# Two experts per token found with VectorE's eight-largest and position-search instructions, on one Trainium2 core

## The reference, cut to what matters

```python
x = x + 0.5 * _L0_ffn_ref(_layernorm(x), ...)    # f0: 8 experts, hidden 176, 2 per token
x = x + _L0_attn_ref(_layernorm(x), ...)         # h: gated linear recurrence
x = x + 0.5 * _L0_ffn_ref(_layernorm(x), ...)    # f0 again
x = x + 0.5 * _L1_ffn_ref(_layernorm(x), ...)    # f1: 16 experts, hidden 128, 2 per token
x = x + _L1_attn_ref(_layernorm(x), ...)         # a: attention
x = x + 0.5 * _L1_ffn_ref(_layernorm(x), ...)    # f1 again
```

```python
scores = sigmoid(x @ gate_w)                # (T, E)
_, idx = top_k(scores + bias, 2)
w = take_along_axis(scores, idx)            # without the bias
w = w / sum(w)                              # f0: clipped at 1e-12; f1: 1e-20 added
```

## Time and profile before

| | |
|---|---|
| median of 3 runs | 845.12 us (844.83 to 847.11) |
| profiled execution, its own time | 842.05 us |
| its span | 840.1 us |
| TensorE busy | 738.6 us (88%) |
| VectorE busy | 481.7 us (57%), 1816 instructions |
| ScalarE busy | 403.6 us (48%) |
| GpSimd busy | 281.0 us (33%) |

### The profile page before, as it was taken

How to read it: one execution, slowest core, us unless ns; L and a number is a source line. 1 busy time by engine, 2 the same in 40 slices (tenths; PEclk the granted TensorE clock), 3 DMA queues, 4 the chain that set the end, 5 groups by cost and what they waited for, 6 DMA issues and landing times.

```text
span 840.1 us, 13928 instructions
## 1 busy us (share of the span) xinstructions
PE 738.6 (88%) x3946; PEld 497.3 (59%) x3946; DVE 481.7 (57%) x1816; ACT 403.6 (48%) x963; POOL 281.0 (33%) x296
## 2 busy tenths in 40 slices
PE   5999999989898999999966899997899888799970
PEld 3446777554465456777543378666667665378640
DVE  5663333478866663333379653335997866753336
ACT  3822433317643722333246436543788777436530
POOL 0572333400000572433306725550011133635550
PEclk9999999999999999999985999999999999899995
DMA  8843333199999943333195245526000011245528
GB/s 301 270 169 119 106 108 104 58 300 351 351 350 350 352 145 119 105 110 105 58 368 219 107 124 166 156 94 200 1 1 1 2 54 41 94 126 171 155 95 300
DMA packets 99295, 134.62 MB, mean 160 GB/s; under 512 B 11494, under 2 KB 88294, under 8 KB 98662
## 3 DMA queue, kind: packets, MB, share of 16 engines
q1 hardware_dynamic: 85782, 95.97, 36.5%
q0 software_dynamic: 13440, 37.77, 12.2%
HBM read 54.85 MB, written 78.84 MB: 159 GB/s over the span
## 4 chain that ended last, share of the span: by engine, by line
PE 66%; DVE 16%; ACT 7%; DMA 4%; issue 4%; POOL 1%; SPq 0%; POOLq 0%; DVEq 0%; ACTq 0%
PE bank L1030 19%; PE bank L1051 11%; PE bank L926 11%; PE bank L1003 4%; PE bank L939 3%; PE bank L1040 3%; PE bank L1113 3%; DVE X L1348 2%; DVE st L1366 2%; DVE X L1352 2%; PE bank L1164 2%; PE bank L866 2%; DMA Y<-f_result_rows 2%; PE bank L1232 1%; PE bank L1140 1%
## 5 line engine op out<-in xcount | busy, mean ns | idle before, releaser
L517 POOL DMA_INDIRECT f_result_rows<-arena x152 | 146.2, 962 | 209.2 <-ACT arena L676 195.5
L517 POOL DMA_INDIRECT slot_rows<-XN,slots x128 | 123.9, 968 | 239.2 <-DVE slots L1480 177.8
L1030 PE MATMUL bank<-w,arena 128*128 (+3 forms) x800 | 176.9, 417 | 2.2 <-ACT arena L661 0.7
L1668 DVE COPY arena<-bank 88x128 f32<-88x128 f32 (+1 forms) x224 | 56.1, 284 | 155.8 <-PE bank L1040 148.7
L1030 PEld LDWEIGHTS bank<-w,arena 128*128 128x128 f32 (+1 forms) x800 | 103.9, 164 | 41.5 <-issue 15.7
L926 PE MATMUL bank<-XT,f_s 128*128 128x512 f32 (+1 forms) x256 | 122.9, 628 | 1.6 <-ACT arena L676 1.0
L1051 PE MATMUL bank<-w,arena 88*128 (+3 forms) x576 | 118.3, 380 | 1.6 <-DVE arena L1668 1.6
L669 ACT ACTIVATE arena<-bank 128x128 f32<-128x128 f32 (+1 forms) x152 | 45.1, 296 | 106.7 <-PE bank L1030 105.7
L676 ACT ACTIVATE arena<-bank 128x256 f32<-128x256 f32 x152 | 58.5, 385 | 59.6 <-PE bank L1051 59.3
L926 PEld LDWEIGHTS bank<-XT,f_s 128*128 128x128 f32 (+1 forms) x256 | 48.3, 197 | 58.5 <-issue 55.7
L1051 PEld LDWEIGHTS bank<-w,arena 88*128 88x128 f32 (+3 forms) x576 | 71.1, 167 | 14.8 <-issue 4.3
(11 more groups left out here) (178 smaller groups left out, 1078.5 us busy)
## 6 DMA issues: line engine op xcount, KB each, us to landing
slot_rows<-zeros SPq DMA_DIRECT2D x16, 2312.0 KB, 20.1
arena<-slot_rows SPq DMA_DIRECT2D x104, 136.0 KB
XN<-f_result_rows SPq DMA_DIRECT2D x32, 256.0 KB, 5.5
Y<-f_result_rows SPq DMA_DIRECT2D x32, 256.0 KB, 6.0
arena<-slot_rows SPq DMA_DIRECT2D x96, 68.0 KB
w<-in_f_w SPq DMA_DIRECT2D x1, 4096.0 KB, 15.7
w<-in_f_w SPq DMA_DIRECT2D x1, 2816.0 KB
f_result_rows<-arena POOLq DMA_INDIRECT x152, 2.4
```

Of the source, the lines that this page charges most:

```text
L517: pool.indirect_dma_start(out=dst, out_offset=bass.IndirectOffsetOnAxis(ap=idx, axis=0), in_=src, in_offset=None).then_inc(done.sem, 16)
L1030: last = pe.matmul(bank[2 + q % 2][lanes, 0:2 * m.H], xsT[q % 2][:, k, lanes], L["w13"][:, k, e, :], start=(k == 0), stop=(k == KD - 1))
L1668: last = dve.tensor_copy(hT[q % 2][0:kp, k, :], bank[4 + q % 2][0:kp, k * P:(k + 1) * P])
```

## The change

The two choices of a token are no longer found one after the other. VectorE's `max` gives the eight largest biased scores of a token in order, `max_index` their positions; both take one tile of 128 tokens at a time, so there are four of each per group, and only the last of the four is waited for. The first two positions are converted to fp32, one comparison marks both choices, and one addition makes the sum for the counts. The owner is copied to `XN` behind it, and is now the expert's number itself, so `lanes` no longer subtracts E and the tables `below` go. In `place` and `weights` both choices are multiplied and reduced by one operation each. The arena grows by 384 columns. In attention, `choose(..., second=False)` now holds the bias addition, the maxima and the searches, and `choose(..., first=False)` the copy, the comparison, the addition and the owner's copy.

```diff
-        ARENA = 14400
+        ARENA = 14784
...
-        ROUTE_STEPS = 101
+        ROUTE_STEPS = 62
...
-                for n in LAYERS:
-                    below_region(n)
...
-                numbers = below[s["kind"]][:, :].unsqueeze(1).broadcast_to((P, GT, E))
...
+                def by_choice(ap, first, tiles):
+                    return ap[:, :, first * E:(first + tiles) * E].rearrange("p k (t e) -> p k t e", e=E)
+                sel, pos = by_expert(f_sel), by_expert(f_pos)
+                both_pos = pos.unsqueeze(1).broadcast_to((P, 2, GT, E))
+                numbers = iota[:, 0:E].unsqueeze(1).unsqueeze(1).broadcast_to((P, 2, GT, E))
...
-                    for k in range(2):
-                        if not (first, second)[k]:
-                            continue
-                        least = f_sum[:, span] if k else XN[:, span, OWNER]
-                        top, one = f_top[:, k, span], by_expert(f_oh[k], g)
-                        chain(dve.tensor_reduce(top, sel, AX.X, ALU.max))
-
-                        chain(dve.tensor_tensor(tmp, sel, over_experts(top), ALU.is_equal))
-                        chain(dve.tensor_tensor(tmp, tmp, numbers, ALU.mult))
-                        chain(dve.tensor_reduce(least, tmp, AX.X, ALU.min))
-                        chain(dve.tensor_tensor(one, numbers, over_experts(least), ALU.is_equal))
-                        if k == 0:
-                            chain(dve.scalar_tensor_tensor(sel, one, -BIG, sel, ALU.mult, ALU.add))
+                        for t in range(GT):
+                            last = dve.max(f_best[:, t, :], sel[:, t, :])
+                        chain(last)
+                        for t in range(GT):
+                            last = dve.max_index(f_rank[:, t, :], f_best[:, t, :], sel[:, t, :])
+                        chain(last)
                     if second:
-                        dve.tensor_tensor(f_m16[:, g, 0:GT * E].rearrange("p (t e) -> p t e", e=E), by_expert(f_oh[0], g),
-                                          by_expert(f_oh[1], g), ALU.add).then_inc(s["both"].sem, 1)
+                        chosen = by_choice(f_oh, GT * g, GT)
+                        chain(dve.tensor_copy(f_pair, f_rank[:, :, 0:2].rearrange("p t k -> p k t")))
+                        chain(dve.tensor_tensor(chosen, numbers, f_pair.unsqueeze(3).broadcast_to((P, 2, GT, E)), ALU.is_equal))
+                        dve.tensor_tensor(f_m16[:, g, 0:GT * E].rearrange("p (t e) -> p t e", e=E), chosen[:, 0], chosen[:, 1],
+                                          ALU.add).then_inc(s["both"].sem, 1)
+                        dve.tensor_copy(XN[:, span, OWNER], f_pair[:, 0, :])
...
-                    for k in range(2):
-                        chain(dve.tensor_tensor(tmp, by_expert(f_oh[k], g), pos, ALU.mult))
-                        chain(dve.tensor_reduce(f_slotf[:, k, span], tmp, AX.X, ALU.add))
+                    chain(dve.tensor_tensor(by_choice(f_tmp, 0, GT), by_choice(f_oh, GT * g, GT), both_pos, ALU.mult))
+                    chain(dve.tensor_reduce(f_slotf[:, :, span], by_choice(f_tmp, 0, GT), AX.X, ALU.add))
...
-                    dve.tensor_scalar(f_lane[:, 0, 0:NT], f_lane[:, 0, 0:NT], float(-E), None, ALU.add)
...
-                    for k in range(2):
-                        chain(dve.tensor_tensor(every, oh[k], score, ALU.mult))
-                        chain(dve.tensor_reduce(tall[:, k, :], every, AX.X, ALU.add))
+                    chain(dve.tensor_tensor(every, by_choice(f_oh, 0, NTT),
+                                            score.unsqueeze(1).broadcast_to((P, 2, NTT, E)), ALU.mult))
+                    chain(dve.tensor_reduce(tall, every, AX.X, ALU.add))
...
-                    for k in range(2):
-                        chain(dve.scalar_tensor_tensor(wts[:, k, :], tall[:, k, :], 0.5, f_sum, ALU.mult, ALU.mult))
+                    chain(dve.scalar_tensor_tensor(wts[:, :, :], tall, 0.5, f_sum.unsqueeze(1).broadcast_to((P, 2, NTT)),
+                                                   ALU.mult, ALU.mult))
```

More of the change, by code:

```diff
@@ L8 @@
 I32 = mybir.dt.int32
+U32 = mybir.dt.uint32
 ALU = mybir.AluOpType
@@ L94, in macaron_kernel @@
         spare = sb("spare", [P, MOE1.TILES])
-        below = {n: sb(n + "_below", [P, m.E]) for n, m in (("f0", MOE0), ("f1", MOE1))}
         region = sb("region", [P, MAXE])
@@ L163, in macaron_kernel @@
         f_sel = c(GT * MAXE)
-        f_tmp = c(GT * MAXE)
-        f_all = c(NTT * MAXE)
-        f_oh = [c(NTT * MAXE), c(NTT * MAXE)]
+        f_best = c(GT, 8)
+        f_rank = c(GT, 8, dt=U32)
+        f_pair = c(2, GT)
+        f_tmp = c(2, GT * MAXE)
+        f_all = c(2, NTT * MAXE)
+        f_oh = c(2, NTT * MAXE)
         f_m16 = c(NG, (GT + 1) * MAXE, dt=F16)
@@ L1309, in constants @@
                 loaded(dve, "const")
-                for n in LAYERS:
-                    below_region(n)
                 dve.tensor_scalar(region[:, :], iota[:, 0:MAXE], float(SPACE), None, ALU.mult).then_inc(numbers_set, 1)
                 dve.tensor_copy(tokens[:, :], tokens16[:, :]).then_inc(numbers_set, 1)
-                dve.wait_ge(numbers_set, 2 + len(LAYERS))
+                dve.wait_ge(numbers_set, 2)
                 dve.tensor_scalar(lane_of[:, :], tokens[:, 0:1], 1.0, None, ALU.subtract).then_inc(numbers_set, 1)
@@ L1318, in constants @@
                 dve.memset(XN[:, :, D:ROW], 0.0).then_inc(numbers_set, 1)
-                dve.wait_ge(numbers_set, 6 + len(LAYERS))
+                dve.wait_ge(numbers_set, 6)
                 dve.tensor_scalar(XN[:, :, TOKEN], tokens[:, :], float(T), None, ALU.add).then_inc(numbers_set, 1)
[L1321 to L1325, removed]
+                dve.wait_ge(numbers_set, 7)
             def shared_add(s, g):
@@ L1555, in weights @@
                 def weights():
-                    tall = f_top
-                    for k in range(2):
-                        chain(dve.tensor_tensor(every, oh[k], score, ALU.mult))
-                        chain(dve.tensor_reduce(tall[:, k, :], every, AX.X, ALU.add))
+                    tall, every = f_top, by_choice(f_all, 0, NTT)
+                    score = f_score[:, 0:NTT * E].rearrange("p (t e) -> p t e", e=E)
+                    chain(dve.tensor_tensor(every, by_choice(f_oh, 0, NTT),
+                                            score.unsqueeze(1).broadcast_to((P, 2, NTT, E)), ALU.mult))
+                    chain(dve.tensor_reduce(tall, every, AX.X, ALU.add))
                     chain(dve.tensor_tensor(f_sum, tall[:, 0, :], tall[:, 1, :], ALU.add))
```

6 lines of the change are left out of this document (removed).

## The result

The changed kernel took 835.24 us (median of 4 runs, 833.39 to 837.43), the kernel before beside it 845.97 us (4 runs, 844.83 to 847.11). The ratio is 0.988, 95% interval 0.986 to 0.991. The forecast of 836.3 us was 1.1 us off, inside its range and inside the likeliest case's own. Against the kernel before beside it the gain is 10.7 us by the medians, where 8.8 were forecast. The ratios in this document leave out executions over 1.5% above the fastest of their kernel, among them two of 1944 us among the 35 of the kernel before that stand beside the first four experiments.

What follows compares the result with a forecast made beforehand. TensorE held most of the wait chain; VectorE savings count only where routing is the chain or TensorE waits. 0.2 + 0.32 + 1.06 + 3.86 + 2.5 + 0.85 = 8.8 us off the median 845.1: 836.3, range 834.0 to 841.7.

Steps and rivals of the forecast that it cites:

- the likeliest case: Whole kernel: the forecast's own case without the rivals, 835 to 838 us, chance 0.50.
- Price of a marking: VectorE's marking of two experts: 3.31 to 2.15 us for 16 experts, 2.88 to 2.01 for 8.
- p: Placing on VectorE: five waited-for operations before the slots become three, 1.02 to 0.64 us, saving 0.38.
- the lower bound: Marking: maxima and searches start 0.07 us apart, as small unwaited aggregations do; savings 1.5 us (16 experts) and 1.2 (8).
- The f0 stages: Marking savings capped by TensorE's waits: 0.32 us in the first f0 stage, 1.06 in the second.
- The first f1 stage: Three markings 3.48 us plus placing 0.38, together 3.86; GpSimd's scatters and SP's row load cap it near 4.5.
- Attention: Marking's first half saves about 1.35 us without GpSimd's hold-up; VectorE 2.1 ahead, then placing 0.38; together 2.5.
- rival 1: Searches held up by GpSimd in attention and slower, about 0.2 us apart: 7.1 us off, 838.0; chance 0.14.
- The last stage: Marking gives 1.16 us, but ScalarE's SILU and copies limit token readiness for TensorE; 0.85 counted.
- Rival 2: Last stage: with 1.9 us idle TensorE's clock may stay up, some 1.4 us more saved: 834.9; chance 0.12.
- edits with one answer: nothing: Stage-end weighting, nine operations to six: some 0.5 us, hidden while VectorE waits for result rows, so counted as nothing.
- if the clock falls where it had not: Sign of failure: TensorE's clock falling at places where it had not fallen before; no size given.

Runs made afterwards that it cites:

- the first four experiments: Marking alone in changed kernel: 0.988 of before; placing and weighting alone on kernel before: 0.994; changed, new marking only in f1: 0.999; changed, every maximum/search waited for: 0.996.
- the pair with 120 fillers: Changed kernel with 120 in place of 90 filler transposes on TensorE ahead of attention, beside the changed kernel: medians 875.78 and 875.73 us.

## Why the prediction was right, and where not

- **Price of a marking**: right. 2.17 us for 16 experts (forecast 2.15) and 1.97 for 8 (265.05 to 267.02; forecast 2.01); placing 0.90 in place of 1.29, p = 0.39 (0.38). The choice to stay near the lower bound, since the operations are small and unwaited, is what decided it: waited for, they cost 0.83 more. Of the Trainium skill's account (Vector Engine (DVE) Microarchitecture Reference, section 3.9) the trace confirms that a search is two instructions. By the 75 ns of section 5.2 there the estimates were 0.09 and 0.18; measured were 0.083 and 0.14 to 0.15.
- **The f0 stages**: right, 0.41 and about 1.0; both waits come back when the marking there is undone.
- **The first f1 stage**: right, 4.12 for 3.86. By the last group's router matmuls (467.48 before, 461.32 now) 3.70 of it was there; 0.8 more came behind them, 0.24 of it by TensorE's clock, and 0.39 went in the wait for rows. GpSimd's and SP's queues became the limit as named, at 4.1 in place of 4.5, since the scatters moved forward by 1.94 and not by 2.6.
- **Attention**: right, 2.2 and 0.6 (0.37 of it the wait for slots) for 2.1 and 0.4, and for the stated reason. A maximum or search is not held up by GpSimd, so rival 1 fell; the run that puts a two-input operation back shows that the relief is not a shift in time. VectorE's scaling came 1.5 us earlier by the first half of the marking, where the forecast counted 1.35 although its own terms (1.80 + 1.10 - 1.39) give 1.51. The Trainium skill's rule (Advanced Engine Details and Errata, DVE and GPSIMD details) agrees with both halves, the 1.12 us beside GpSimd's addition and the 0.68 of the four searches beside it.
- **The last stage**: 1.15 at the positions, and 0.98 at the router matmuls for which the forecast had 0.85 (719.49 and 713.07, less the lead of 5.44). The 2 us behind them are TensorE's clock (router and shared matmuls 1.08 + 5.16 before, 0.64 + 3.60 now), and some 0.6 went again where TensorE waits for rows. Rival 2's effect appeared, but its mechanism is not borne out: the same kernel lost the clock on another chip (5.64) after a shorter wait, and 2.85 us of wait kept it elsewhere. No run shows that these 2 us belong to the change.
- **Weighting, "edits with one answer: nothing"**: this step failed. It was costed by what covers VectorE, not by what it does to GpSimd. The merged product holds up the scatter beside it for 0.27 us longer at the two f1 ends, where the last scatters are on the path: at most 0.5 us in all. The cover, too, is that of the f1 ends: moved behind the landing it stood on the path after the second f0 stage.
- **-3.65 at attention's start**: up to 0.27 is the weighting's. 2.4 are the clock (projections and transposes 3.78 + 3.78 + 1.18 against 3.38 + 1.99 + 0.93). Transposes and queries stood as low in the run with placing and weighting alone, which has the old marking (1.19 and 3.39). The keys vary in the changed kernel itself, 3.78 in its second and 1.99 in its third profiled execution; over all traces with 90 fillers they were low five times of ten with the new marking and not in the two with the old, so a part of the change in this is neither shown nor excluded. About 1.2 us is the idle time, 4.42 for 3.23, over the landing of rows; it was 4.22 with before's marking and 3.97 in another execution of the changed kernel. No row shows that the change brings it. Of the 1.0 up to the recurrence's end 0.7 are of the same kind (four matmuls 1.98 in place of 2.66). Of the 0.9 at the end up to 0.27 is the weighting's, and 0.65 stand between the first loads of result rows and the end (820.78 to 840.1 before, 813.03 to 833.0 now).
- **A sign of failing that did show**: "if the clock falls where it had not". It did, for the keys at attention's start (1.99 to 3.78) and for the last router matmuls of the first f1 stage (0.64 to 1.08). The total came out all the same because the clock gave back about as much elsewhere; this part of the match is luck.

So the forecast terms came to 0.41 + 1.01 + 4.12 + 2.82 + 0.98 = 9.3 us, less up to 0.5 for the weighting, for the 8.8 foretold. In this profiled execution the terms that were not forecast took some 2 us of it away; over the medians (10.7 us, with an interval of 8 to 12) they did not.

## What to carry to other kernels

A chain of small waited-for operations is paid in waits: here six of them cost 0.14 us each, and per-tile instructions that follow each other unwaited gave three quarters of what a marking saves, although there are more instructions. Before costing an edit at nothing, ask not only what hides it but whom it holds up: a longer two-input VectorE operation beside GpSimd delays GpSimd. Compare a clock-dependent stretch over several executions of one kernel before giving it to a change. And where two spans differ by what was expected, look at which place the difference arises: in the pair with 120 fillers it did not arise where it should.

## What the runs showed of the hardware

- Eight-largest over 128x16 and 128x8: 0.164 and 0.156 us alone, 0.083 and 0.07 apart when unwaited. Load and search: 0.08 and 0.17, a pair every 0.14 to 0.15.
- GpSimd and VectorE's two-input operations can each hold the other up: an addition took 1.12 for 0.23 beside GpSimd's addition; an indirect scatter that starts beside a product took 1.47 (128x512) or 1.20 (128x256), and 0.96 without one.
- TensorE's clock can be at 1.2 or 2.4 GHz at the same place of the same kernel in different executions (here on different chips): eight shared matmuls 3.60 and 5.64 after waits of 1.64 and 1.62. After 2.9 to 4.4 us of idle time the query projection ran wholly or mostly low (3.38 to 3.78) twelve times of twelve; after 0.7 us or none, high (1.99) both times.
- The kernel before took 846 us on one chip and 880 to 889 on three others, with the ratio of changed kernel to it the same (0.988, and 0.988 and 0.990 on two of them). Why is not shown.
